# One activation table set for exponential and logarithm in a decoder layer kernel

## What is computed

```python
x = x + attn(layernorm(x))            # 32 heads of 32, 8 key/value heads, rotary, causal softmax
x = x + xattn(layernorm(x), ctx, ctx) # correlation by FFT, the 9 largest lags, softmax, sum of shifted values
x = x + ffn(layernorm(x))             # below

# ffn, per token: 24 logits -> a 4x4 matrix and two vectors of 4
H_pre, H_post = softmax(...), softmax(...)
Z = H_res_logits / 0.1
for _ in range(50):                   # Sinkhorn
    u = -logsumexp(Z + v[None, :], -1)
    v = -logsumexp(Z + u[:, None], -2)
H_res = exp(Z + u[:, None] + v[None, :])
out = H_res' @ streams + H_post * ((H_pre @ streams) @ W_branch)
```

## Time and profile before

| | |
|---|---|
| median of three executions | 1248.21 us |
| the profiled execution's own time | 1247.06 us |
| its span, first to last instruction | 1245.1 us |
| mean granted TensorE clock | 0.916 of full |
| busy: PE, DVE, ACT, POOL | 83%, 75%, 52%, 40% |
| attention, autocorrelation, mixing begin at about | 0, 635, 1109 us |
| table loads on ACT | 25 |

### The profile page before, as it was taken

How to read it: one execution, slowest core, us unless ns; L and a number is a source line. 1 busy time by engine, 2 the same in 40 slices (tenths; PEclk the granted TensorE clock), 3 DMA queues, 4 the chain that set the end, 5 groups by cost and what they waited for, 6 DMA issues and landing times. The chain is left out here.

```text
span 1245.1 us, 23491 instructions
## 1 busy us (share of the span) xinstructions
PE 1029.9 (83%) x7928; PEld 781.0 (63%) x7928; DVE 932.4 (75%) x2818; ACT 641.3 (52%) x1827; POOL 492.4 (40%) x684
## 2 busy tenths in 40 slices
PE   5699999999999999999648999999887995615056
PEld 4577777787777777777436677767665663313034
DVE  6766787666678666666507778779998998897994
ACT  6434555544455544445516677778567655323133
POOL 2523443333343333344324666666565542201020
PEclk9799999999999999999679999999999997657578
DMA  9011011111101111110132123223222211139025
GB/s 377 25 42 57 19 57 57 57 57 40 45 28 57 57 57 57 40 41 19 58 120 85 68 83 117 89 77 123 73 81 81 73 39 38 43 120 332 0 56 131
DMA packets 47235, 95.72 MB, mean 77 GB/s; under 512 B 5952, under 2 KB 30400, under 8 KB 47168
## 3 DMA queue, kind: packets, MB, share of 16 engines
q1 hardware_dynamic: 47168, 94.91, 22.9%
HBM read 64.48 MB, written 27.26 MB: 74 GB/s over the span
## 5 line engine op out<-in xcount | busy, mean ns | idle before, releaser
L613 POOL TENSOR_TENSOR prob_G<-prob_G,rl 128x512 f32<-128x512 f32 x96 | 99.8, 1040 | 258.2 <-DVE rl L501 258.2
L383 ACT ACTIVATE prob_G<-prob_G,negm 128x128 f32<-128x128 f32 x384 | 148.8, 389 | 89.5 <-DVE negm L443 89.5
L244 PE MATMUL ps_qkv<-w_hi,xT_hi 128*128 128x512 f32 x384 | 156.7, 408 | 13.5 <-DVE prob_G L506 8.6
L245 PE MATMUL ps_qkv<-w_lo,xT_hi 128*128 128x512 f32 x384 | 151.4, 394 | 0.0
L246 PE MATMUL ps_qkv<-w_hi,xT_lo 128*128 128x512 f32 x384 | 151.2, 394 | 0.0
L316 PE MATMUL ps_qkv<-wo_hi,aT_hi 128*128 128x512 f32 x256 | 107.7, 421 | 0.0
L318 PE MATMUL ps_qkv<-wo_hi,aT_lo 128*128 128x512 f32 x256 | 102.1, 399 | 0.0
L317 PE MATMUL ps_qkv<-wo_lo,aT_hi 128*128 128x512 f32 x256 | 101.9, 398 | 0.0
L244 PEld LDWEIGHTS ps_qkv<-w_hi,xT_hi 128*128 128x128 f32 x384 | 73.2, 191 | 39.0 <-issue 16.1
L439 DVE TENSOR_TENSOR prob_G<-ps_s,mask 128x512 f32<-128x512 f32 x96 | 65.0, 677 | 41.4 <-PE ps_s L227 40.8
L468 DVE TENSOR_TENSOR xT_lo<-ps_t,xT_hi 128x512 fp32r<-128x512 f32 x16 | 11.1, 693 | 104.2 <-ACT xT_hi L422 104.2
(11 more groups left out here) (246 smaller groups left out, 2819.6 us busy)
## 6 DMA issues: line engine op xcount, KB each, us to landing
xin<-in_x SPq DMA_DIRECT2D x16, 512.0 KB, 3.3
xres<-in_x SPq DMA_DIRECT2D x16, 512.0 KB, 5.0
x<-xres SPq DMA_DIRECT2D x16, 512.0 KB, 2.6
c_xin<-x SPq DMA_DIRECT2D x16, 512.0 KB, 4.9
c_cin<-in_ctx SPq DMA_DIRECT2D x16, 512.0 KB, 4.2
c_b_xres<-x SPq DMA_DIRECT2D x16, 512.0 KB, 3.3
rows_x<-c_row SPq DMA_DIRECT2D x64, 128.0 KB, 2.3
m_xm<-rows_x SPq DMA_DIRECT2D x16, 512.0 KB, 8.6
```

Source lines behind the costliest of these rows:

```text
L244: nc.tensor.matmul(ps_qkv[:, n, :], xT_hi[:, k, :], w_hi[:, k, cols], start=k == 0, stop=False)
L245: nc.tensor.matmul(ps_qkv[:, n, :], xT_hi[:, k, :], w_lo[:, k, cols], start=False, stop=False)
L383: r = nc.scalar.activation(prob(g)[:, j, :], prob(g)[:, j, :], ACT.Exp, bias=negm[:, h:h + 1], accum_out=lsum[:, h:h + 1])
L613: nc.gpsimd.tensor_tensor(prob(g), prob(g), rl[:, g * GROUP:(g + 1) * GROUP].rearrange("p (j o) -> p j o", o=1).to_broadcast([P, GROUP, T] ...
```

## The change

One instruction is put at the head of ACT's stream in the first phase. It loads the table set that holds exponential and logarithm together. Nothing else is edited.

```diff
         @block.scalar
         def _(act):
+            nc.scalar.preload_act_table_set("natural_log_exp_and_others")
             act.wait_ge(const_in, 48)
```

## The result

The changed kernel took **1232.66 us** at the median of four executions (1232.33 to 1233.24), beside 1248.28 for the kernel before (1247.65 to 1251.31). The ratio is 0.9871, with a 95% interval of 0.9854 to 0.9888. A second series of five executions gave 1235.36 (1232.62 to 1236.79) beside 1248.56, a ratio of 0.9884 (0.9864 to 0.9904): a gain of 13.2 us. The profiled executions, 1247.06 and 1233.24 us with spans of 1245.1 and 1231.4, differ by 13.8 us. What needs explaining is thus 13 to 16 us, not 10.7.

A forecast was written before the change was run, and what follows sets the result against it. No engine bounds it throughout (PE busy 83%, DVE 75%, ACT 52%); ACT's loads count only where another engine waits. Gains of 1.28 + 3.20 + 1.28 + 2.09 + 0.80 + 1.28 + 0.73 = 10.66 us gave 1237.5 us, range 1233.5 to 1242.1.

The forecast's parts named there:

- rival 4: Whole kernel: loads still placed at each change of function; 1248.2 us, or 1246.9 if only the start gains; chance 0.04.
- rival 5: Attention turns: combined set lacks a function such as Copy, adding up to 38.5 us on ACT, so slower; chance 0.02.
- Start: First load moves into ACT's idle wait for constants, so ACT, DVE and PE start sooner; gain 1.28 us.
- Turn 6 into 7: Weight spectrum starts 1.47 us sooner and PE's full clock saves another 1.73; gain 3.20 us.
- Turn 11: DVE's wait for chain a's two logarithms loses one load; gain 1.28 us, upper bound 1.97.
- Rival 1: PE's clock does not follow, in turn 7 or elsewhere; 1239.2 us, or 1240.8 with two more falls; chance 0.22.
- Turn 14 to the mixing: Four loads in turn 14 into 15 gain 2.09 us; chain c's last exponential in turn 17 gains 0.80.
- Mixing: Chain b's first logarithms come 1.28 us sooner and chain c's last exponential 0.73; DVE's chain paces the 88 us between.
- Rival 2: The gain at the start is absorbed by the weights' transfers; 1238.8 us; chance 0.10.
- Rival 3: Each removed switch also frees a drain, 1.38 us more at each of seven places; 1227.8 us; chance 0.02.
- Places: Experiments' theory: each load costs what its place shows, covered loads nothing, and part of turn 7 is PE's clock.
- landing: Rival theory in the experiments: clock falls and transfers fell favourably in the new timing as a whole.

The follow-up runs named there:

- experiment 3: Changed kernel with two loads put back ahead of chain a's operations 2 and 3 (turn 6 into 7); 1237.28 us, ratio 0.9912.
- experiment 5: Changed kernel with its two loads of turn 11 put back, ahead of chain a's operations 6 and 8; 1236.45 us, ratio 0.9907.
- experiment 9: Chain b's first logarithms issued ahead of the evictions of rows 0 and 1, in the changed kernel (1230.43 us) and in the kernel before (1241.29 us).
- experiment 1: Kernel before with only its first table load moved to the head of ACT's stream, the other 24 loads kept; 1246.03 us, ratio 0.9987.
- experiment 7: Changed kernel with four loads of the mixing put back, ahead of chain b's operations 6, 8, 11 and chain c's 11; 1238.97 us, ratio 0.9905.
- experiment 8: Changed kernel with loads put back at all 14 places on or next to the path, covered ones left out; 1247.78 us, ratio 0.9983.
- experiment 2: Also the two "late" kernels: changed kernel with its one load back behind the first transpose's wait, sampled twice; 1238.15 and 1236.29 us.
- experiment 4: Changed kernel with the eleven loads put back that had been priced at nothing as covered; 1235.02 us, ratio 0.9888.

## Why the prediction was right or wrong

Direction and mechanism were right, and so were the small chances of rivals 4 and 5: there is one load, and all functions are in one set. The sum was too low, above all in the mixing (2.01 us forecast, 4.53 measured), and the range too narrow; its lower end adds up to 1233.4, not 1233.5. Step by step, in the profiled execution, against the forecast in brackets:

- **Start: 1.03 us at the first product, 0.60 by turn 6 (1.28).** The step "ACT, DVE and PE start 1.28 us sooner" failed. Next late was PE's second transpose, for which the second `xT_hi` waits, and not the weights' transfers that I had looked at. The idle time of PE shows it: 4.88 became 3.90. What was lost between the first product and turn 6 is not explained: the profiled executions differ there from 0.13 to -1.86 us, with one and the same code behind the start.
- **Turn 6 into 7: 3.30 (3.20).** Right in both parts, and experiment 3 shows both. The gap was to be 0.59 us and was 0.44.
- **Turn 11: 1.58 (1.28).** DVE's wait fell by 1.42 and not by 1.28, towards the upper bound of 1.97; experiment 5 took back 1.59. The other 0.16 us lie in the stretch behind it, where I had assumed nothing.
- **Turns 12 to 14: 0.52 (0).** "Ends of turns 8 to 13 should keep their distances" was wrong by a slow stretch of the clock that moved. Before, the window 1014 to 1019 of turn 13 has a clock of 0.66, and none from 983 to 987; after, one stands at 983 to 987:

```profile
983.00:987.00 4.00, 4.00 (x14) 3.19 (x13) 3.65 (x9) 3.01 (x5) 2.75 (x10) 0.57 0.38 131
```

  It cost 0.41 us in turn 12 and gave 0.93 in turn 13. No load is behind it: the kernel before with the new order of experiment 9, which has all its loads, has the same -0.41 and 0.93, and experiments 1 and 5 have neither. So this 0.52 us is luck. Rival 1 named it ("falls may come or go"), with the wrong sign.
- **Turn 14 to the mixing: 3.13 (2.09 + 0.80 = 2.89).** Right. Of it 2.26 us came in turn 14 into 15 and 0.86 in turn 17; the idle times came to 0.44, 0.21 and 0 as forecast. The transfer of `m_gt` that opens the mixing came at 1100.33, where 1100.8 was forecast.
- **Mixing: 4.53 (1.28 + 0.73 = 2.01).** This is the step that failed most. It has five parts. The transfers ahead of row 0 were 0.66 us shorter; I had priced them at nothing, and that was luck: from the transfer of `m_gt` to row 0 it took 13.56 us before and 12.90 after, but 12.65 in experiment 1, with all loads. Up to the first logarithms 1.84 came in: the load of 1.28, and 0.39 of the time from row 0 to row 1 (5.39 us became 5.00). From there to the second logarithms 0.23. To chain c's last exponential 1.02, where 0.73 was forecast. Then 0.78 for the last rows, where nothing was: PE waited less ahead of them, its first one fell from 3.75 to 3.57 us and the small product behind it from 1.15 to 0.74, nearly all in the clock. "From there DVE's chain sets the pace" left out that PE's rows set it too, at one of two clocks: directly at the last rows, and through ACT's evictions ahead of chain c's logarithms (experiment 7). How much of the 4.53 is the change and how much the draw can be estimated: the seven profiled executions with no load in the mixing gained 1.48 to 4.68 us there, 3.5 on average, and the two with every load and the old order 0 (the one before) and 0.57 (experiment 1). That leaves some 3 us for the change, an estimate, where 2.01 was forecast.
- **Profiled to median: I added 1.15 us to get from the execution before to its median.** The changed kernel's profiled execution lay 0.6 above its median instead, so 1.8 of the 15.6 us is in no stretch; with 13.2 us of gain the second series doesn't have them. Single executions of the kernel before went from 1243.60 to 1254.12, and 1.15 was one draw of that. The second series, with 2.4 us less gain, has its median inside the range.

The terms add up: 10.66 forecast - 0.68 (start, with its loss up to turn 6) + 0.11 (turn 7 and on) + 0.30 (turn 11) + 0.52 (turns 12 to 14) + 0.24 (turn 14 to mixing) + 2.52 (mixing) = 13.67 us.

**The rivals.** Rival 2, absorption at the start, came true for 0.30 of the 1.28 us at the first product, but by PE's second transpose and not by the weights' transfers. Rival 3, that each switch frees a further 1.38 us, is against the runs: taking two loads back at turn 11 cost 1.59 us and four at turn 14 cost 1.94, less than the loads themselves (2.57 and 5.13 us). The loads put back load one and the same set, so the kernel before has to speak for real switches: its waits at these places, 2.24, 1.71 and 1.02 us, are those with the loads put back (2.25, 1.72 and 1.02). In the traces a load and the activation behind it are 0.01 to 0.02 us apart, as in the earlier trace rows. The Trainium skill (ScalarE: Activation LUTs, "What ACT_TABLE_LOAD costs") counts a drain of about 1380 ns beside each switch. No run here shows it, and the runs decide for the bare 1283 ns. Rival 1 in turn 7 did not come true; elsewhere the clock was more than half of the 3.0 us of error: 0.52 in turns 12 to 14, 0.39 in the first rows of the mixing and 0.78 in the last.

**Places or landing?** Taking back each group, in medians against the mean gain of the changed kernel's two series, (15.6 + 13.2) / 2 = 14.4 us, costs 2.9 us for the start (mean of its two samples), 2.8 for turn 7, 0.5 for the covered ones, 1.0 for turn 11, 2.4 for turn 14 and 3.5 for the mixing. These add to 13.1 us, and turn 17's load, which was only tried with the others, has 0.86 us in the trace. But each has an uncertainty of 3 to 5 us from its interval, so none of these prices is clear of it by medians alone. Two things carry "places": the three stretches of the table that come and go with their own loads to within 0.1 us (but for the one 3.56), and experiment 8, in whose ten executions the 14 loads take back all of the gain but 2.1 us (0.2 to 3.9). "Landing" holds for how far one series, or one execution, differs from another, and not as an effect of the loads: the two "late" kernels and the code ahead of experiment 7's loads show such differences without any. What stays open is the price of the start, 1.0 us at PE's wait and 2.9 by medians, the price of the mixing within some 2 us, and whether the clock falls more often when loads are left; that would take many profiled executions of each.

## What to carry to other kernels

Where an engine alternates between functions of different table sets, count the switches, then price each one by the wait that ends behind it: 25 loads of 1.28 us were 32.1 us of ACT and 13 to 16 us of time. Look at what the removed wait uncovers, and by how little a load is covered (0.11 us ahead of chain c's logarithms): a producer one step further back, a slow clock that goes with the idle gap, an eviction that stands ahead of the operation (placing the logarithms first gave another 2 to 5 us). A stretch that differs between two executions of the same code can't price a change from one pair of them. A range built from one profiled execution should be at least as wide as the kernel's own executions are apart.

## What was not expected of the hardware

- One `p_out` row of 8 products took 1.97 us at the 2.4 GHz level and up to 3.78 at 1.2 GHz, and which rows of the mixing were slow differed from run to run. In the second row of chain a it was slow in three profiled kernels (experiments 3, 4 and 8) and of chain b in five (the first of 2, 7, 8 and both of 9); the two kernels of experiment 2 do the same work and differ in it. Such a row took 1.6 to 1.8 us more than the others, and the rows after it moved by as much.
- In turn 7 a clock of 0.72 over 6 us went with 2.06 and 2.07 us of idle time on PE ahead of it, and 1.00 with 0.44. The same product after it took 5.40 and 3.70 us.
- A table set can hold exponential, logarithm, copy and square together, and loading it cost the same 1283 ns as the narrower ones.
